# The attention layer of a two-layer graph network: its edge networks' steps in another order, and four waits of GpSimd inside a chunk's gathers

## Chip, cores and metric

One NeuronCore of a Trainium2 chip runs the whole program in one launch. The metric is the device time of one execution in microseconds, the median of the runs shown.

## What is computed

A graph of N = 6250 nodes with D = 64 features and E = 206,250 edges, sorted by target row, goes through two layers, each behind a layer norm and a ReLU: a gated relation layer (`_L0_gnn_ref`), and an attention layer. All is float32. The change touches the attention layer alone; cut to that:

```python
def ssp(x): return softplus(x) - log(2)
row, col = edge_index
W_k = lin(ssp(lin(edge_attr, wkn_w1, wkn_b1)), wkn_w2, wkn_b2)   # the key network, 32 -> 16 -> 16
W_v = lin(ssp(lin(edge_attr, wvn_w1, wvn_b1)), wvn_w2, wvn_b2)   # the value network, 32 -> 16 -> 16
keys_j = lin(W_k[:, None, :] * h_keys[col], wkl_w, wkl_b)
qk_ij = sum(h_queries[row] * keys_j, axis=-1)
alpha = segment_softmax(qk_ij, row, n)                           # over the edges of one row
msg_j = lin(W_v[:, None, :] * h_values[col], wvl_w, wvl_b)
aggr = segment_sum(alpha[:, :, None] * msg_j, row, num_segments=n)
out = lin(ssp(lin(x, cen_w, cen_b) + aggr), out_w, out_b)
```

The kernel folds the linear parts behind the networks into node tables, so that an edge needs the gathered row of its column (keys and values, 128 floats), its network outputs (32 floats) and its row's query.

## The kernel before, in words

The program runs in stages, one behind the other: a front, a sort of the edge records (`sort`, some 130 to 2880 us), the relation layer and its nodes, `attention_layer` (3399 to 5712 us) and `attention_nodes`.

**Tiling.** Each of the 128 partitions holds a run of consecutive edges. They are taken in CHUNKS = 62 chunks of T = 26 edges for each partition. The loop goes over PAIRS = 31 pairs; in each body b = 0, 1 and n = 2i + b. First and last pair are written out, the 29 between are a hardware loop (`loop`, L100). Tiles with [b] are double buffered.

**What a chunk costs each engine in the attention layer.**
- SP loads the chunk's attributes (attr) and query starts (qin), L1376 and L1378.
- GpSimd issues 26 indirect DMAs (L1395), each a gather of 128 rows of kv_table into one column of got[b]. Before the first it waits for s_used (DVE is done with got[b] of chunk n-2), s_idx (the indices of n) and s_w (TensorE has turned the networks' output of chunk n-1). A `sem_inc` on k.s_passed stands behind such waits.
- TensorE computes the networks of chunk n: transposes of flat_attr into p_a (L1411, signal s_at), a product with w1 into p_z (L1416, s_z), one with w2 into p_a again (L1420, s_net), and the turn back into p_w (L1424, s_w). The work is in two halves of 4 and 3 groups of 128 columns; between two steps ACT or DVE has one: ACT's copies to attr_t (L1452), its relu, abs, exp and ln (L1456 to L1460, signal s_soft), DVE's add relu + soft (L1530, s_ssp), ACT's copy with bias to net_t (L1467, s_net_copied).
- DVE takes the chunk through the attention: a scan that spreads queries over edges (L1537), product with the gathered keys (L1545, behind its waits for s_w and s_got), with the key network (L1548), sum by head (L1549), a running maximum (L1557) and differences (below, L1563, signal s_below), value times value network (L1567, s_value), times the weight (L1572, behind its wait for ACT's s_exp), and the scan of the state (L1580, s_state).
- ACT lays out queries (L1437) and marks (L1442), takes exponentials (L1472 to L1475), packs the results (L1479, L1483) and issues their store (L1486).

**Order around the change.** The order on each engine is written by hand. In ACT's body for n stand: lay_out(n+1), networks(n+1) from flat_attr to ln, then finish(n): exponentials, networks_end(n+1), packing, marks(n+1), store. DVE has activated(n+1) behind L1567 and ahead of L1572. TensorE's body for n holds the four steps of chunk n's networks one behind the other.

In the sort stage GpSimd issues 26 scatters for a chunk (L625). From the third chunk on it also waits at each fourth of them for s_dst, a step of TensorE (L623).

## Time and profile before

| | us |
|---|---|
| median of 3 runs | 5864.14 |
| lowest and highest | 5855.48, 5867.09 |
| profiled execution, its own time | 5865.56 |
| its span | 5863.7 |
| granted TensorE clock, mean of the span | 0.531 |
| attention layer, from GpSimd's first gather to DVE's last state scan | 3399.8 to 5709.1 |
| busy in the span: PE, DVE, ACT, GpSimd | 2726.4, 3881.4, 2758.0, 3278.9 |

Times in the profile are microseconds from the start of the span. PE is TensorE, DVE VectorE, ACT ScalarE, POOL GpSimd and SP SyncE; PEld are TensorE's weight loads. A timeline row gives start, length, engine, line, what is written from what, and in brackets the engine's idle time before it with what ended that: an instruction, "issue" where nothing in the profile ended just then, "remote" where a semaphore update arrived that no instruction's end stands close to. Most signals reach their waiter within 0.1 us of the end of the instruction that sends them. Ends of matmuls are modelled.

### The profile page before, as it was taken

To read this page: it belongs to the slowest core of one execution; us is meant where nothing else is said; L and a number is where in the kernel's file an instruction comes from. 1 tells how busy PE (TensorE), PEld (TensorE's weight loads), DVE (VectorE), ACT (ScalarE), POOL (GpSimd) and SP (SyncE) were. 2 spreads that over 40 slices of the span, in tenths; PEclk is the share of its full clock that TensorE was granted. 3 is DMA by queue.
4 is the path that set the end of the run, shared out by engine and by line. 5 is a ranking of instruction groups with operands and counts; after the bars stand their busy time and mean duration, and the time that the engine had idled before them with its cause. 6 is when DMAs were issued, how large, how long until landed. Compare 5 with 4: busy or idle time off the path is not lost. (4 is left out here: it accounts for less than half of the span.)

```text
span 5863.7 us, 79660 instructions
## 1 busy us (share of the span) xinstructions
PE 2726.4 (46%) x21110; PEld 1693.1 (29%) x21111; DVE 3881.4 (66%) x8751; ACT 2758.0 (47%) x5413; POOL 3278.9 (56%) x3388
## 2 busy tenths in 40 slices
PE   7655555555555555555488622322223222222223
PEld 7433333333333333333388511111111111111102
DVE  9867777777777777776599645655556666655552
ACT  3244444444444444444122345655555555555552
POOL 0146565666666565656610266666666666666653
PEclk8555555555555555555577755555555555555555
DMA  5112121212121212121477533433334343433321
GB/s 64 55 54 71 63 71 62 71 63 71 63 71 63 71 63 71 63 71 58 103 160 145 72 103 100 124 110 108 108 103 111 109 110 103 110 108 109 109 79 24
DMA packets 691304, 505.28 MB, mean 86 GB/s; under 512 B 588446, under 2 KB 605214, under 8 KB 691109
## 3 DMA queue, kind: packets, MB, share of 16 engines
q1 hardware_dynamic: 573012, 246.99, 18.2%
q0 software_dynamic: 108736, 196.93, 11.6%
q10 hardware_dynamic: 9360, 59.56, 2.7%
q14 instruction: 172, 1.40, 0.1%
q8 instruction: 24, 0.39, 0.0%
HBM read 289.96 MB, written 213.26 MB: 86 GB/s over the span
## 5 line engine op out<-in xcount | busy, mean ns | idle before, releaser
L625 POOL DMA_INDIRECT records<-rec,place x1612 | 1557.2, 966 | 1306.9 <-issue 451.0
L1395 POOL DMA_INDIRECT got_a<-kv_table,idx_a x1612 | 1539.5, 955 | 762.8 <-issue 691.9
L860 DVE SCALAR_TENSOR_TENSOR same_before<-p_src,src_f,before 128x128 bf16<-128x128 f32 x1612 | 775.0, 535 | 0.0
L711 ACT ACTIVATE lo_away<-p_lo,minus_number 128x512 bf16<-128x512 f32 x434 | 291.2, 671 | 615.5 <-remote 593.6
L668 PE MATMUL p_src<-fields,select 3*128 3x512 bf16 x434 | 248.3, 572 | 687.7 <-DVE same_before L860 512.0
L1411 PE MATMUL p_a<-ident,flat_attr 128*128 128x128 f32 x434 | 123.5, 433 | 930.5 <-issue 447.4
L807 DVE TENSOR_TENSOR picked<-p_look,hi_hot 128x392 f32<-128x392 f32 x434 | 231.5, 533 | 407.5 <-remote 398.2
L1420 PE MATMUL p_a<-relu,w_t 128*128 128x512 f32 x248 | 230.8, 1034 | 463.4 <-issue 332.5
L850 DVE TENSOR_SCALAR dst_hot<-p_dst,number 128x512 bf16<-128x512 f32 x434 | 307.3, 708 | 191.1 <-remote 178.1
L643 PE MATMUL p_look<-table_low,lo_hot_t 128*128 128x98 bf16 x1612 | 410.2, 281 | 0.0
L643 PE MATMUL p_look<-table_rest,lo_hot_t 128*128 128x98 bf16 x1612 | 409.4, 280 | 0.0
L1545 DVE TENSOR_TENSOR prod<-got_a,wide 128x1664 f32<-128x1664 f32 x62 | 117.0, 1888 | 440.2 <-remote 216.3
L643 PE MATMUL p_look<-table,lo_hot_t 128*128 128x98 bf16 x1612 | 402.3, 278 | 0.0
L730 ACT ACTIVATE h_gated<-p_h,gate_s 128x64 f32<-128x64 f32 x1586 | 372.1, 315 | 51.5 <-remote 12.2
L653 PE MATMUL p_h<-window,dst_hot 128*128 128x64 bf16 x4836 | 357.6, 242 | 65.1 <-issue 64.9
L1014 PE MATMUL acc<-high,lo_r 128*128 128x64 bf16 x1708 | 345.4, 244 | 60.0 <-DVE low L1079 40.7
L708 ACT COPY table<-p_place 128x49 f32<-128x49 f32 x434 | 91.7, 211 | 597.0 <-issue 371.6
L1411 PEld LDWEIGHTS p_a<-ident,flat_attr 128*128 128x128 f32 x434 | 75.6, 215 | 978.3 <-issue 824.4
L1014 PE MATMUL acc<-rest_r,lo_r 128*128 128x64 bf16 x1708 | 344.3, 243 | 0.0
L1014 PE MATMUL acc<-low,lo_r 128*128 128x64 bf16 x1708 | 344.2, 243 | 0.0
L653 PEld LDWEIGHTS p_h<-window,dst_hot 128*128 128x128 bf16 x4836 | 312.2, 133 | 54.2 <-issue 53.8
L1014 PEld LDWEIGHTS acc<-high,lo_r 128*128 128x128 bf16 x1708 | 291.3, 171 | 67.6 <-issue 66.3
(377 smaller groups left out, 8443.3 us busy)
## 6 DMA issues: line engine op xcount, KB each, us to landing
sums<-packed_a ACTq DMA_DIRECT2D x62, 936.0 KB
q_starts<-zero_q SPq DMA_DIRECT2D x62, 884.0 KB
rec_r<-records SPq DMA_DIRECT2D x124, 442.0 KB
qin<-q_starts SPq DMA_DIRECT2D x62, 884.0 KB
attr_a<-records SPq DMA_DIRECT2D x62, 442.0 KB
records<-rec,place POOLq DMA_INDIRECT x1612
got_a<-kv_table,idx_a POOLq DMA_INDIRECT x1612
stage<-in_edge_attr SPq DMA_DIRECT2D x61, 416.0 KB
```

Source lines behind the costliest of these rows:

```text
L625: nc.gpsimd.indirect_dma_start(k.records, bass.IndirectOffsetOnAxis(ap=place[b][:, t:t + 1], axis=0), rec[b][:, t, :], None).then_inc(s_se ...
L643: last = nc.tensor.matmul(p_look[qb][:, j * 2 * HI:(j + 1) * 2 * HI], lo_hot_t[qb][:, j * P:(j + 1) * P], part, start=(e == 0), stop=(e == 2))
L653: last = nc.tensor.matmul(p_h[qb][:, j * D:(j + 1) * D], dst_hot[qb][:, j * P:(j + 1) * P], part, start=(e == 0), stop=(e == 2))
L668: nc.tensor.matmul(p_src[:, 0:m * P], k.select[:, NODE, :], rows, start=True, stop=True).then_inc(s_src, 1)
L711: nc.scalar.activation(lo_away[qb][:, 0:m * P], p_lo[:, 0:m * P], ACT.Abs, bias=k.minus_number[:]).then_inc(s_lo_away, 1)
L730: last = nc.scalar.activation(to, p_h[qb][:, j * D:(j + 1) * D], ACT.Copy, scale=gate[b][:, t:t + 1])
L807: v.tensor_tensor(picked[:, 0:n, :, :], p_look[gb][:, 0:n * 2 * HI].rearrange("p (g a h) -> p g a h", a=2, h=HI), bc(group_hot(k, b, g, HI ...
L850: v.tensor_scalar(dst_hot[qb][:, 0:m * P], p_dst[:, 0:m * P], k.number[:], None, ALU.is_equal).then_inc(s_dst_hot, 1)
L860: last = v.scalar_tensor_tensor(same_before[:, first:first + j + 1, :].rearrange("p g e -> p (g e)"), p_src[:, 0:(j + 1) * P], k.src_f[:, ...
L1014: last = nc.tensor.matmul(acc[:, to(t // SUPER)], lo[b][:, :, t], part, start=False, stop=True, skip_group_check=True)
L1395: nc.gpsimd.indirect_dma_start(got[b][:, t, :], None, k.kv_table, bass.IndirectOffsetOnAxis(ap=idx[b][:, t:t + 1], axis=0)).then_inc(s_got ...
L1420: nc.tensor.matmul(p_a[:, 0:c1 - c0], k.w2_t[:], relu[:, c0:c1], start=True, stop=True).then_inc(s_net, 1)
```

## The change

TensorE's steps become four functions of a chunk number m: attributes (the transposes), first_product, second_product and turned (the turn back). The body for n now holds second_product(n+1), attributes(n+2), turned(n+1), first_product(n+2). The banks p_a and p_z become p_n[0] and p_n[1], one for each half, and each is used for all three kinds of output of its half. The prologue computes the networks of chunk 0 and part of those of chunk 1.

ACT's order for n becomes: lay_out(n+1), networks_end(n+1), flattened(n+2), exponentials(n), attributes(n+2), and in finish(n), behind the wait for s_state: marks(n+1), activation(n+2), packing, store. DVE's activated moves from between L1567 and L1572 to ahead of the waits for s_w and s_got, and its one add over 896 columns becomes seven over 128, with s_ssp raised once a half.

GpSimd loses the wait for s_w ahead of a chunk. From the second pair on it waits ahead of gather 4 for s_net of chunk n, ahead of 8 for s_at of n+1, ahead of 13 for s_w of n, and ahead of 18 for s_z of n+1, each with a `sem_inc` on k.s_passed behind it. `follows(i, b, more)` tells whether chunk n + more exists.

```diff
--- before.py
+++ after.py
@@ -1347,7 +1347,7 @@
         relu = tile("relu", [P, GROUPS * P])
         soft = tile("soft", [P, GROUPS * P])
         half = tile("half", [P, 1])
-        p_a, p_z = bank("p_a"), bank("p_z")
+        p_n = [bank(f"p_n{j}") for j in range(2)]
         p_w = banks("p_w", 2)
         wide = banks("wide", 4)
         flat = wide[:, 0:QW * T1]
@@ -1360,6 +1360,10 @@
         s_rec, s_qin, s_got, s_store = ([sem(f"{n}{b}") for b in range(2)] for n in ("s_rec_a", "s_qin", "s_got_a", "s_store_a"))
         records_v, starts_v, sums_v = by_run(k.records), by_run(k.q_starts), by_run(k.sums1)
 
+        def follows(i, b, more):
+
+            return not (isinstance(i, int) and 2 * i + b + more >= CHUNKS)
+
         halves = ((0, 4 * P, 4), (4 * P, GROUPS * P, GROUPS - 4))
 
         with nc.Block() as block:
@@ -1389,9 +1393,18 @@
                         n = 2 * i + b
                         wait(pool, s_used, n - 1)
                         pool.wait_ge(s_idx, n + 1)
-                        wait(pool, s_w, n)
                         pool.sem_inc(k.s_passed, 1)
                         for t in range(T):
+                            if not (isinstance(i, int) and i == 0) and t in (4, 8, 13, 18):
+                                if t == 4:
+                                    pool.wait_ge(s_net, 2 * n + 2)
+                                if t == 8 and follows(i, b, 1):
+                                    pool.wait_ge(s_at, 2 * n + 4)
+                                if t == 13:
+                                    pool.wait_ge(s_w, n + 1)
+                                if t == 18 and follows(i, b, 1):
+                                    pool.wait_ge(s_z, 2 * n + 4)
+                                pool.sem_inc(k.s_passed, 1)
                             nc.gpsimd.indirect_dma_start(
                                 got[b][:, t, :], None, k.kv_table,
                                 bass.IndirectOffsetOnAxis(ap=idx[b][:, t:t + 1], axis=0)).then_inc(s_got[b], 16)
@@ -1400,29 +1413,50 @@
 
             @block.tensor
             def _(pe):
+                def attributes(m):
+                    pe.wait_ge(s_flat, m + 1)
+                    wait(pe, s_net_copied, 2 * m)
+                    for j, (c0, c1, groups) in enumerate(halves):
+                        for g in range(c0 // P, c0 // P + groups):
+                            last = nc.tensor.transpose(p_n[j][:, g * P - c0:(g + 1) * P - c0], flat_attr[:, g * G:(g + 1) * G, :].rearrange("p t c -> p (t c)"), k.ident[:])
+                        last.then_inc(s_at, 1)
+
+                def first_product(m):
+                    for j, (c0, c1, groups) in enumerate(halves):
+                        pe.wait_ge(s_at_copied, 2 * m + j + 1)
+                        nc.tensor.matmul(p_n[j][:, 0:c1 - c0], k.w1_t[:], attr_t[:, c0:c1], start=True, stop=True).then_inc(s_z, 1)
+
+                def second_product(m):
+                    for j, (c0, c1, groups) in enumerate(halves):
+                        pe.wait_ge(s_ssp, 2 * m + j + 1)
+                        pe.wait_ge(s_z_read, 2 * m + j + 1)
+                        nc.tensor.matmul(p_n[j][:, 0:c1 - c0], k.w2_t[:], relu[:, c0:c1], start=True, stop=True).then_inc(s_net, 1)
+
+                def turned(m):
+                    wait(pe, s_value, m)
+                    pe.wait_ge(s_net_copied, 2 * m + 2)
+                    for g in range(GROUPS):
+                        last = nc.tensor.transpose(p_w[:, g * P:(g + 1) * P], net_t[:, g * P:(g + 1) * P], k.ident[:])
+                    last.then_inc(s_w, 1)
+
+                attributes(0)
+                first_product(0)
+                second_product(0)
+                attributes(1)
+                turned(0)
+                first_product(1)
+
                 def body(i):
                     for b in range(2):
                         n = 2 * i + b
-                        pe.wait_ge(s_flat, n + 1)
-                        for j, (c0, c1, groups) in enumerate(halves):
-                            wait(pe, s_at_copied, 2 * n + j)
-                            wait(pe, s_net_copied, 2 * n)
-                            for g in range(c0 // P, c0 // P + groups):
-                                last = nc.tensor.transpose(p_a[:, g * P - c0:(g + 1) * P - c0], flat_attr[:, g * G:(g + 1) * G, :].rearrange("p t c -> p (t c)"), k.ident[:])
-                            last.then_inc(s_at, 1)
-                        for j, (c0, c1, groups) in enumerate(halves):
-                            pe.wait_ge(s_at_copied, 2 * n + j + 1)
-                            wait(pe, s_z_read, 2 * n + j)
-                            nc.tensor.matmul(p_z[:, 0:c1 - c0], k.w1_t[:], attr_t[:, c0:c1], start=True, stop=True).then_inc(s_z, 1)
-                        pe.wait_ge(s_ssp, n + 1)
-                        for j, (c0, c1, groups) in enumerate(halves):
-                            wait(pe, s_net_copied, 2 * n + j)
-                            nc.tensor.matmul(p_a[:, 0:c1 - c0], k.w2_t[:], relu[:, c0:c1], start=True, stop=True).then_inc(s_net, 1)
-                        wait(pe, s_value, n)
-                        pe.wait_ge(s_net_copied, 2 * n + 2)
-                        for g in range(GROUPS):
-                            last = nc.tensor.transpose(p_w[:, g * P:(g + 1) * P], net_t[:, g * P:(g + 1) * P], k.ident[:])
-                        last.then_inc(s_w, 1)
+                        if follows(i, b, 1):
+                            second_product(n + 1)
+                        if follows(i, b, 2):
+                            attributes(n + 2)
+                        if follows(i, b, 1):
+                            turned(n + 1)
+                        if follows(i, b, 2):
+                            first_product(n + 2)
 
                 loop(pe, body)
 
@@ -1441,20 +1475,26 @@
                     act.wait_ge(s_same, n + 1)
                     nc.scalar.copy(factor[:, :, 1:T1], bc(same[b][:], 1, QW)).then_inc(s_keep, 1)
 
-                def networks(n, i, b):
+                def flattened(n, i, b):
 
                     act.wait_ge(s_rec[b], 16 * (i + 1))
                     wait(act, s_at, 2 * n)
                     nc.scalar.copy(flat_attr[:, 0:T, :], attr[b][:, :, 0:EC]).then_inc(s_flat, 1)
+
+                def attributes(n):
+
                     wait(act, s_z, 2 * n)
                     for j, (c0, c1, _) in enumerate(halves):
                         act.wait_ge(s_at, 2 * n + j + 1)
-                        nc.scalar.copy(attr_t[:, c0:c1], p_a[:, 0:c1 - c0]).then_inc(s_at_copied, 1)
+                        nc.scalar.copy(attr_t[:, c0:c1], p_n[j][:, 0:c1 - c0]).then_inc(s_at_copied, 1)
+
+                def activation(n):
+
                     wait(act, s_net, 2 * n)
                     for j, (c0, c1, _) in enumerate(halves):
                         act.wait_ge(s_z, 2 * n + j + 1)
-                        nc.scalar.activation(relu[:, c0:c1], p_z[:, 0:c1 - c0], ACT.Relu, bias=k.b1_c[:])
-                        nc.scalar.activation(soft[:, c0:c1], p_z[:, 0:c1 - c0], ACT.Abs, bias=k.b1_c[:]).then_inc(s_z_read, 1)
+                        nc.scalar.activation(relu[:, c0:c1], p_n[j][:, 0:c1 - c0], ACT.Relu, bias=k.b1_c[:])
+                        nc.scalar.activation(soft[:, c0:c1], p_n[j][:, 0:c1 - c0], ACT.Abs, bias=k.b1_c[:]).then_inc(s_z_read, 1)
                     act.wait_ge(s_z_read, 2 * n + 2)
                     c.then(nc.scalar.activation(soft[:], soft[:], ACT.Exp, scale=-1.0))
                     nc.scalar.activation(soft[:], soft[:], ACT.Ln, bias=half[:], scale=0.5).then_inc(s_soft, 1)
@@ -1464,22 +1504,25 @@
                     wait(act, s_w, n)
                     for j, (c0, c1, _) in enumerate(halves):
                         act.wait_ge(s_net, 2 * n + j + 1)
-                        nc.scalar.activation(net_t[:, c0:c1], p_a[:, 0:c1 - c0], ACT.Identity, bias=k.b2_c[:]).then_inc(s_net_copied, 1)
-
-                def finish(n, i, b):
+                        nc.scalar.activation(net_t[:, c0:c1], p_n[j][:, 0:c1 - c0], ACT.Identity, bias=k.b2_c[:]).then_inc(s_net_copied, 1)
+
+                def exponentials(n):
 
                     act.wait_ge(s_below, n + 1)
                     nc.scalar.activation(add[:, D:QW, 1:T1], below[:], ACT.Exp)
                     nc.scalar.activation(weight, below[:], ACT.Exp)
                     nc.scalar.activation(factor[:, 0:D, :].rearrange("p (h d) t -> p h d t", h=NH), bc(drop[:], 2, HD), ACT.Exp)
                     nc.scalar.activation(factor[:, D:QW, :], drop[:], ACT.Exp).then_inc(s_exp, 1)
-                    if not at_end(i, b):
-                        networks_end(n + 1)
+
+                def finish(n, i, b):
+
+                    act.wait_ge(s_state, n + 1)
+                    if follows(i, b, 1):
+                        marks(n + 1, i + b, 1 - b)
+                    if follows(i, b, 2):
+                        activation(n + 2)
                     wait(act, s_store[b], 16 * i)
                     c.mark(nc.scalar.copy(packed[b][:, :, QW:SW], top[b][:, :, 1:T1].rearrange("p h t -> p t h")))
-                    act.wait_ge(s_state, n + 1)
-                    if not at_end(i, b):
-                        marks(n + 1, i + b, 1 - b)
                     nc.scalar.copy(packed[b][:, :, 0:QW], state[b][:, :, 1:T1].rearrange("p c t -> p t c")).then_inc(s_packed, 1)
                     act.wait_ge(s_packed, n + 1)
                     c.wait()
@@ -1489,17 +1532,27 @@
                 c.begin(0)
                 marks(0, 0, 0)
                 lay_out(0, 0, 0)
-                networks(0, 0, 0)
+                flattened(0, 0, 0)
+                attributes(0)
+                activation(0)
                 networks_end(0)
+                flattened(1, 0, 1)
+                attributes(1)
+                activation(1)
 
                 def body(i):
                     if not at_start(i):
                         c.begin(i)
                     for b in range(2):
                         n = 2 * i + b
-                        if not at_end(i, b):
+                        if follows(i, b, 1):
                             lay_out(n + 1, i + b, 1 - b)
-                            networks(n + 1, i + b, 1 - b)
+                            networks_end(n + 1)
+                        if follows(i, b, 2):
+                            flattened(n + 2, i + 1, b)
+                        exponentials(n)
+                        if follows(i, b, 2):
+                            attributes(n + 2)
                         finish(n, i, b)
                     if not at_end(i):
                         c.end()
@@ -1527,7 +1580,11 @@
 
                 def activated(n):
                     dve.wait_ge(s_soft, n + 1)
-                    nc.vector.tensor_tensor(relu[:], relu[:], soft[:], ALU.add).then_inc(s_ssp, 1)
+                    for j, (c0, c1, groups) in enumerate(halves):
+                        for g in range(groups):
+                            at = slice(c0 + g * P, c0 + (g + 1) * P)
+                            last = nc.vector.tensor_tensor(relu[:, at], relu[:, at], soft[:, at], ALU.add)
+                        last.then_inc(s_ssp, 1)
 
                 def chunk(n, i, b):
                     dve.wait_ge(s_query, n + 1)
@@ -1539,6 +1596,8 @@
                     dve.wait_ge(s_q, n + 1)
                     c.then(nc.vector.tensor_copy(query[1 - b][:, :, 0:1], factor[:, :, T:T1]))
 
+                    if follows(i, b, 1):
+                        activated(n + 1)
                     dve.wait_ge(s_w, n + 1)
                     dve.wait_ge(s_got[b], SCATTERED * (i + 1))
 
@@ -1565,8 +1624,6 @@
                     value = got[b][:, :, D:2 * D]
                     by_head = value.rearrange("p t (h d) -> p t h d", h=NH)
                     nc.vector.tensor_tensor(by_head, by_head, bc(nets[:, :, HD:EC], 2, NH), ALU.mult).then_inc(s_value, 1)
-                    if not at_end(i, b):
-                        activated(n + 1)
                     dve.wait_ge(s_exp, n + 1)
                     dve.wait_ge(s_value, n + 1)
                     nc.vector.tensor_tensor(add[:, 0:D, 1:T1].rearrange("p (h d) t -> p h d t", h=NH), value.rearrange("p t (h d) -> p h d t", h=NH),
```

## Rows read from the trace of the kernel before

**Rows 1.** The page's costliest groups: GpSimd's gathers. Columns: busy, mean ns, idle before.

```profile
L1395 POOL DMA_INDIRECT got_a<-kv_table,idx_a x1612 | 1539.5, 955 | 762.8 <-issue 691.9
```

**Rows 2.** The windows view, steady part of the attention layer. Columns: stretch, length, engines, PEclk.

```profile
3806.00:5584.00 1778.00, 516.75 (x1056) 221.37 (x1056) 1057.98 (x1009) 1004.05 (x1009) 1187.97 (x1248) 0.50 0.40 109
```

**Rows 3.** The timeline of GpSimd: start, length, work, idle time before and its releaser.

```profile
3399.75 0.96 POOL L1395 DMA_INDIRECT got_a<-kv_table,idx_a  x1 [11.44 <-DVE idx_a L1518]
...
4431.95 0.95 POOL L1395 DMA_INDIRECT got_a<-kv_table,idx_a  x1 [0.30 <-issue]
...
4464.11 0.94 POOL L1395 DMA_INDIRECT got_a<-kv_table,idx_a  x1 [0.30 <-issue]
4472.77 0.94 POOL L1395 DMA_INDIRECT got_a<-kv_table,idx_a  x1 [7.72 <-issue]
...
5584.30 0.95 POOL L1395 DMA_INDIRECT got_a<-kv_table,idx_a  x1 [9.46 <-issue]
```

**Rows 4.** The timeline of all engines, chunk 28, second after a stop of GpSimd.

```profile
4453.79 1.73 PE L1424 MATMUL p_w<-ident,net_t 128*128 128x128 f32 x7 [1.14 <-issue]
...
4468.19 1.09 PE L1411 MATMUL p_a<-ident,flat_attr 128*128 128x128 f32 x4 [12.67 <-issue]
...
4472.10 0.59 ACT L1452 COPY attr_t<-p_a 128x512 f32<-128x512 f32 x1 [4.14 <-remote]
4472.18 1.89 DVE L1545 TENSOR_TENSOR prod<-got_a,wide 128x1664 f32<-128x1664 f32 x1 [8.51 <-remote]
```

**Rows 5.** The same view, chunk 27, first after a stop.

```profile
4401.47 1.92 PE L1416 MATMUL p_z<-attr_t,w_t 128*128 128x512 f32 x2
...
4403.48 0.69 ACT L1456 ACTIVATE relu<-p_z,b_c 128x512 f32<-128x512 f32 x1 [1.29 <-PE p_z L1416]
```

**Rows 6.** The same view, chunk 28, half way.

```profile
4438.31 1.62 PE L1416 MATMUL p_z<-attr_t,w_t 128*128 128x384 f32 x2 [1.88 <-ACT soft L1457]
...
4442.46 0.58 ACT L1456 ACTIVATE relu<-p_z,b_c 128x384 f32<-128x384 f32 x1 [4.29 <-remote]
```

**Rows 7.** The same view, sort stage, its second chunk, which has no wait inside.

```profile
311.63 0.96 POOL L625 DMA_INDIRECT records<-rec,place  x1 [34.45 <-ACTq L762]
...
316.46 0.28 PE L643 MATMUL p_look<-table_low,lo_hot_t 128*128 128x98 bf16 x1
...
343.25 0.96 POOL L625 DMA_INDIRECT records<-rec,place  x1 [0.30 <-issue]
348.40 0.57 DVE L807 TENSOR_TENSOR picked<-p_look,hi_hot 128x392 f32<-128x392 f32 x1 [23.92 <-remote]
```

**Rows 8.** The timeline of GpSimd, sort stage: the first scatter of four runs.

```profile
1107.72 0.96 POOL L625 DMA_INDIRECT records<-rec,place  x1 [2.51 <-remote]
...
1120.29 0.96 POOL L625 DMA_INDIRECT records<-rec,place  x1 [2.64 <-remote]
...
1129.98 0.96 POOL L625 DMA_INDIRECT records<-rec,place  x1 [2.40 <-PE p_dst L670]
...
1136.62 0.96 POOL L625 DMA_INDIRECT records<-rec,place  x1 [1.89 <-PE p_dst L670]
```

**Rows 9.** The timeline of DVE behind chunk 28's first gather.

```profile
4433.27 1.89 DVE L1545 TENSOR_TENSOR prod<-got_a,wide 128x1664 f32<-128x1664 f32 x1 [5.48 <-DMA got_a<-kv_table,idx_a]
...
4440.61 1.88 DVE L1567 TENSOR_TENSOR got_a<-got_a,p_w 128x1664 f32<-128x1664 f32 x1
```

**Rows 10.** The view of waits, attention layer: us in total, times, longest.

```profile
DVE relu L1530 <- ACT soft L1460: 167.0, 46, 19.8
```

**Rows 11.** Groups of instructions, attention layer: busy, mean ns, idle before.

```profile
L1530 DVE TENSOR_TENSOR relu<-relu,soft 128x896 f32<-128x896 f32 x62 | 67.8, 1094 | 255.1 <-ACT soft L1460 167.0 <-issue 88.1
...
L1563 DVE TENSOR_TENSOR below_a<-logit_carry,top 128x104 f32<-128x104 f32 x62 | 16.6, 268 | 2.1
```

**Rows 12.** The timeline of all engines, chunk 28: an add of DVE and a gather.

```profile
4446.88 1.09 DVE L1530 TENSOR_TENSOR relu<-relu,soft 128x896 f32<-128x896 f32 x1 [4.39 <-ACT soft L1460]
4447.10 1.70 POOL L1395 DMA_INDIRECT got_a<-kv_table,idx_a  x1 [0.31 <-issue]
```

## The prediction

> **What bounds the kernel now.** I began with the page: 26 gathers for each of 62 chunks make 1,612 issues by GpSimd at L1395, 955 ns each, and the idle time before them is mostly "issue" [rows 1]. The windows view of the steady part of the attention layer, 3806 to 5584 us, is 48 chunks: GpSimd 1187.97 us busy, DVE 1057.98, ACT 1004.05, PE 516.75 [rows 2]. That is 24.7, 22.0, 20.9 and 10.8 us for a chunk. Then GpSimd's own timeline: it begins the layer at 3399.75 and chunk 59 at 5584.30, so 37.03 us for a chunk [rows 3]. Back to back a gather takes 1.25 us (0.95 busy, 0.30 between), 26 of them 32.5. The missing 4.5 us is no steady loss: chunk 27's gathers run into chunk 28's at 4431.95 with 0.30 us between, the last starts at 4464.11, and chunk 29's first only at 4472.77 [rows 3]. After every 52 gathers there is one stop of 7 to 9.5 us. GpSimd's pace sets the stage; what ends that stop sets GpSimd.
>
> **What ends the stop.** The timeline of all engines shows it [rows 4]. TensorE's transposes into p_w (s_w of chunk 28) end at 4455.5. GpSimd and DVE both wait for that semaphore, and both go on only at 4472.2 to 4472.8, DVE after 8.51 us idle "remote" (an update came, but no instruction had ended just then). In the same moment ACT's L1452 starts at 4472.10 after transposes that ended at 4469.3. So work of TensorE is done and its word reaches nobody for up to 16 us. In the first chunk after a stop the word comes at once: matmuls end at 4403.4, ACT starts at 4403.48 [rows 5]. In the second, L1416 ends at 4439.93 and ACT starts at 4442.46, 2.5 us late [rows 6]. No wait of this kind stands behind ACT's or DVE's work.
>
> The sort stage shows the same on another kernel body. Its second chunk issues 26 scatters with no wait inside, 311.63 to 344.2; TensorE's L643 had ended by 316.8, and DVE takes it up at 348.40, 4.2 us after GpSimd is done [rows 7]. Later chunks wait after 4 to 8 scatters, and GpSimd's runs of 8, 6 and 4 start 12.57, 9.69 and 6.64 us apart [rows 8]. With the 74.07 us for 52 of [rows 3] the four lie near one line, 1.02 us for a run and 1.405 us for each gather in it (8 gives 12.3, 6 gives 9.5). I read it so: once a signal of TensorE is held back, it comes out only when GpSimd has been idle for 0.15 us per gather of the run, and a wait on it costs a run its 1.02 us on top.
>
> **The change, part by part.**
> 1. GpSimd's wait on s_w at a chunk's head goes; waits on s_net, s_at, s_w, s_z come at gathers 4, 8, 13 and 18. Queued behind each are the rest of that chunk's gathers, and for the last of them waits DVE's L1545. If the step is done and its signal is out, a wait costs nothing: the one at 4431.95 stands behind a gap of 0.30 us like any other [rows 3]. Are the steps done? Chunk 28's gathers begin at 4431.95, DVE's L1545 of the chunk before at 4433.27, its L1567 ends at 4442.5 [rows 9]; TensorE's turn takes 1.73 [rows 4], so s_w is ready 12.3 us after the first gather, and gather 13 starts at 16.3. s_z comes after ACT's exponentials and copies and L1416's passes (1.92 and 1.62 us, [rows 5, 6]); I put it some 5 us behind s_w, at 17, against gather 18 at 22.5. s_net and s_at come earlier by 4 us or more against theirs, since DVE will be waiting for gathers. So a stop comes only from a held signal.
> 2. second_product for n+1, attributes for n+2, turned for n+1 and first_product for n+2 run in the body of n, a chunk further ahead. In ACT's order the activation of n+2 moves behind the state scan, where L1572's wait on ACT does not see it. The work is the same; two table loads for a chunk stay. DVE's path from one L1545 to the next loses L1530's wait for ACT (167.0 us in 46 chunks, 19.8 at most, [rows 10]) and comes to an estimated 28 us: 22.0 busy [rows 2] and some 6 us of waits for ACT (mark, soft, exponentials). That is worth nothing while GpSimd needs 37, and is needed if GpSimd came down to 32.5.
> 3. L1530, 896 columns in 1,094 ns, becomes seven adds of 128. By that rate and by a 104-column operation's 268 ns [rows 11] they take 1.1 to 1.9 us on DVE, in front of L1545 now, where DVE waits for gathers anyway: nothing, 1.9 at worst if GpSimd ceased to bind. A gather beside L1530 took 1.70 us in place of 0.95 [rows 12]; 0.75 us for a chunk is the most that smaller pieces give back. I take nothing, the two cancelling and the stops setting the rate. SBUF — State Buffer of the Trainium skill (section SBUF: two separate sides) has it that a DVE operation with two SBUF inputs and a GpSimd one that reads SBUF lock each other out for a whole instruction. By that a gather could lose the whole 1.09 us; the row shows 0.75 once, not at each.
> 4. SP's loads wait on s_flat and s_query, whose order on ACT changes, not their count; no DMA is added. The prologue does two chunks' networks and GpSimd's first two chunks have no waits inside. Between 10 us lost and 5 won, once; I take 0.
>
> **The sum.** Everything hangs on how many stops a chunk has, by the line above: one in two chunks 37.05 us, one per chunk 37.55, two 38.56, four 40.6. Today it is one in two. In the first chunk of a run signals came at once, in the second they came late; so a run of much over 26 gathers ends in a held one, and with a wait every 4 to 8 gathers GpSimd meets it at once rather than at the chunk's end. I take between one and two, 1.5: 26 x 1.405 + 1.5 x 1.02 = 38.06, 1.03 more than 37.03. The first two chunks have no waits inside, so 60 x 1.03 = +62 us. The sum is made against the profiled run, 5865.6 (span 5863.7 and 1.9 around it): 5927.4. The median of the runs, 5864.14, is 1.4 below that run, so I name 5926.
>
> **The rivals.**
> - **No signal is held: GpSimd back to back.** For it: after a stop signals were prompt for a whole chunk [rows 5], GpSimd now pauses its queue four times a chunk, and DVE (28) and ACT (21) fit below. Against it: in [rows 4] the queue had been waiting and the signal still stayed away until the engine had been idle for 7 us. It needs 32.5 us a chunk: (37.03 - 32.5) x 62 = 281 less, 5583; with a stop in one run of three or so, or late starts, up to 5750. Chance 0.27, with its partial forms. TensorE: Matmul & The Clock Gate of the Trainium skill (section The cost: per-tile semaphore tail) prices a matmul's semaphore increment at 26.3 ns behind a tail of about 25 ns, with nothing that depends on other engines; by it this rival would be the forecast, and [rows 4, 7] disagree with it by 4 to 16 us.
> - **Every wait is a stop, as in the sort stage** [rows 8]. Decides if a signal is held in most runs of six gathers. 40.6 us a chunk, +222: 6086. For it: the sort's signals are late in runs of 4. Against it: the attention layer's are not in the first 26. Chance 0.13.
> - **One stop in two chunks, as now.** The held signal is the same s_w, caught at gather 13 and not at the head; 37.05 a chunk, nothing changes: 5855 to 5875. Chance 0.10.
> - **The waits at the forecast's rate**, one or two stops for a chunk: 5885 to 5990. Chance 0.50.
>
> **How the numbers follow.** Faster by over 0.2% (12 us, about what a measurement here can tell from no change) is the first rival and a few of the forecast's edges: 0.29. Same: 0.10. Slower: 0.61. Left out of the range are the purest form of the first rival and the worst of the second: 5630 to 6080; the slower cases alone would span 5885 to 6086.
>
> **What would show it.** L1395's starts: stops per chunk, and run length against time on the line 1.02 + 1.405 n. Forecast right: stops of 3 to 6 us at gathers 4, 8, 13 or 18, most at one place; the stop at each second chunk's head gone; DVE's L1545 still waiting for gathers; L1572's wait for ACT gone. First rival: gaps of 0.30 us through whole chunks, and DVE no longer waiting "remote". Wrong altogether: a run far off the line, a stop that a late step of TensorE explains (its matmul ends just before), or DVE's path at over 33 us.

## The result, and the profile after

| | before | after |
|---|---|---|
| median of 20 runs each | 5864.13 | 5876.82 |
| lowest and highest | 5848.01, 5879.48 | 5860.05, 5890.16 |
| ratio, 95% interval | | 1.0027 [1.0017, 1.0036] |
| profiled execution, its own time and span | 5865.56, 5863.7 | 5890.16, 5888.4 |
| layer, first gather to end of the last state scan | 3399.75 to 5709.08: 2309.3 | 3410.09 to 5734.38: 2324.3 |

The kernel is slower, by 12.7 us, where the forecast had 62. The layer itself is 15.0 longer in the profiled runs. All that lies ahead of it also moves with no edit there: the layer's first gather is 10 us later here, and between 3379 and 3473 in the profiles of the experiments on like chips. So times of the layer are read from its own first gather on.

The page's groups after (columns as in [rows 1]):

```profile
L1408 POOL DMA_INDIRECT got_a<-kv_table,idx_a x1612 | 1526.1, 947 | 791.1 <-issue 492.1
...
L1433 PE MATMUL p_n<-relu,w_t 128*128 128x512 f32 x248 | 206.8, 989 | 745.0 <-DVE relu L1586 524.9
...
L1604 DVE TENSOR_TENSOR prod<-got_a,wide 128x1664 f32<-128x1664 f32 x62 | 117.0, 1888 | 587.6 <-DMA got_a<-kv_table,idx_a 516.9
```

The windows view of 48 chunks, to be set against [rows 2] (columns as there):

```profile
3835.00:5612.00 1777.00, 463.84 (x1056) 238.15 (x1056) 1075.39 (x1292) 983.83 (x1008) 1177.18 (x1244) 0.55 0.40 108
```

GpSimd's gathers keep it busy 13 us less (1526.1 against 1539.5), the idle time before them is 28 us more (791.1 against 762.8), and 48 chunks take the same time, 1777 against 1778. DVE waits for gathers (516.9 us), as the prediction said. Its idle time ahead of the product with the weight, which stands behind the wait for ACT's s_exp, fell from 147 to 31 us, where the prediction had that wait gone. What GpSimd waits for is in the view of waits, 3430 to 5720 (us in total, times, longest):

```profile
DVE prod L1604 <- DMA got_a<-kv_table,idx_a: 516.9, 51, 16.5
...
POOL got_a L1408 <- remote: 265.6, 58, 8.8
...
ACT relu L1496 <- remote: 112.0, 33, 11.4
ACT attr_t L1489 <- remote: 107.0, 24, 7.8
...
POOL got_a L1408 <- PE p_n L1433: 18.6, 2, 18.3
```

58 stops end "remote", that is with a held signal, and one of 18.3 us with work of TensorE. GpSimd's timeline shows the kinds: a stop in each chunk in the first third, then mostly one or two in every second chunk:

```profile
3630.53 0.94 POOL L1408 DMA_INDIRECT got_a<-kv_table,idx_a  x1 [4.41 <-remote]
3667.34 0.94 POOL L1408 DMA_INDIRECT got_a<-kv_table,idx_a  x1 [4.51 <-remote]
...
5284.85 0.94 POOL L1408 DMA_INDIRECT got_a<-kv_table,idx_a  x1 [6.90 <-remote]
5294.10 0.94 POOL L1408 DMA_INDIRECT got_a<-kv_table,idx_a  x1 [3.31 <-remote]
```

From 3630.53 to 3667.34 there are 26 gathers and one stop: 36.81 us, 1.416 for each. The prediction's line gives 37.55. In the kernel before, the 25 runs of 52 gathers from 3733.06 to 5584.30, with one stop each, cost 74.05, 1.424 for each gather. After, 52 gathers with three stops, from 3742.25 to 3816.34, cost 74.09; the line gives 76.12. **In this layer and on these chips the added stops cost nothing.** The held signals are as large as before: for the stop that ends at 5284.85 GpSimd waits for transposes that ended at 5272.74.

The difference lies at the start. Heads of chunks 0, 3 and 60 on GpSimd are at 3399.75, 3506.88, 5616.80 before and at 3410.09, 3527.43, 5641.33 after. So the first three chunks take 107.1 and 117.3, **10.2 more**; the next 57 take 2109.9 and 2113.9, 4.0 more, 37.02 against 37.09 for a chunk. The rest, 0.8, is at the end. Two more traces of the changed kernel (f1 and g1 below) have 117.4 and 117.2 for the first three chunks and 36.92 and 37.11 for a chunk behind them. So the loss at the start repeats, and the 4.0 is no more than these traces differ among themselves; of the kernel before there is one trace. The 10.2 is this stop (the timeline of all engines, after):

```profile
3473.93 0.48 ACT L1489 COPY attr_t<-p_n 128x384 f32<-128x384 f32 x1 [7.76 <-remote]
...
3478.80 0.94 POOL L1408 DMA_INDIRECT got_a<-kv_table,idx_a  x1 [0.30 <-issue]
...
3487.31 0.69 ACT L1496 ACTIVATE relu<-p_n,b_c 128x512 f32<-128x512 f32 x1 [11.36 <-remote]
...
3492.95 1.50 DVE L1586 TENSOR_TENSOR relu<-relu,soft 128x128 f32<-128x128 f32 x7 [12.58 <-ACT soft L1500]
...
3493.91 3.35 PE L1433 MATMUL p_n<-relu,w_t 128*128 128x512 f32 x4 [17.80 <-DVE relu L1586]
...
3498.05 0.94 POOL L1408 DMA_INDIRECT got_a<-kv_table,idx_a  x1 [18.30 <-PE p_n L1433]
```

GpSimd has issued 56 gathers without a wait and stands ahead of gather 4 of chunk 2 for s_net. What is held is not s_net but two earlier signals, s_at's second half and s_z, on ACT's side. ACT gets s_z only 8.5 us after the last gather's start, and behind it stand ACT's activation, DVE's adds and the second product: 10.7 us of real work, to 3498.05.

### The profile page after: what moved, and what is told of

Same layout as the page of the kernel before. It is cut to its first block and busy times, and to the rows that moved or that the text cites. A ratio compares the mean times of both kernels' runs of the same rounds, so it can differ in the third digit from the quotient of the medians.

```text
span 5888.4 us, 80298 instructions
## 1 busy us (share of the span) xinstructions
PE 2656.3 (45%) x21110; PEld 1713.9 (29%) x21111; DVE 3909.9 (66%) x9123; ACT 2735.1 (46%) x5413; POOL 3260.6 (55%) x3388
## 5 line engine op out<-in xcount | busy, mean ns | idle before, releaser
L625 POOL DMA_INDIRECT records<-rec,place x1612 | 1552.5, 963 | 1323.5 <-issue 444.8
L1408 POOL DMA_INDIRECT got_a<-kv_table,idx_a x1612 | 1526.1, 947 | 791.1 <-issue 492.1
L1433 PE MATMUL p_n<-relu,w_t 128*128 128x512 f32 x248 | 206.8, 989 | 745.0 <-DVE relu L1586 524.9
L1604 DVE TENSOR_TENSOR prod<-got_a,wide 128x1664 f32<-128x1664 f32 x62 | 117.0, 1888 | 587.6 <-DMA got_a<-kv_table,idx_a 516.9
L1439 PE MATMUL p_w<-ident,net_t 128*128 128x128 f32 x434 | 108.7, 428 | 536.5 <-issue 295.5
L1433 PEld LDWEIGHTS p_n<-relu,w_t 128*128 128x128 f32 x248 | 72.8, 324 | 866.0 <-DVE relu L1586 580.0
```

What stands on the lines that cost most here:

```text
L625: nc.gpsimd.indirect_dma_start(k.records, bass.IndirectOffsetOnAxis(ap=place[b][:, t:t + 1], axis=0), rec[b][:, t, :], None).then_inc(s_se ...
L1408: nc.gpsimd.indirect_dma_start(got[b][:, t, :], None, k.kv_table, bass.IndirectOffsetOnAxis(ap=idx[b][:, t:t + 1], axis=0)).then_inc(s_got ...
L1433: nc.tensor.matmul(p_n[j][:, 0:c1 - c0], k.w2_t[:], relu[:, c0:c1], start=True, stop=True).then_inc(s_net, 1)
```

## The experiments

The prediction's theory, P: a stop costs GpSimd 1.02 us on top of 1.405 for each gather. What was found instead, A: on these chips GpSimd cannot keep 1.25 us for a gather in the long run; it falls behind a slower rate, and a stop only makes up for that and costs nothing. The text calls this the backlog. Each batch had its own runs of the kernel before beside it.

### What does a chunk cost without any wait for TensorE?

**e1**, the kernel before with networks for chunk 0 alone:

```diff
-                        wait(pool, s_w, n)
...
-                loop(pe, body)
+                body(0)
...
-                            networks(n + 1, i + b, 1 - b)
+                            flattened(n + 1, i + b, 1 - b)
```

> The kernel before, but TensorE computes the edge networks of chunk 0 alone and every chunk uses that output; ACT's and DVE's network steps of later chunks are left out, and so is each wait on TensorE after chunk 0. Held signals (theory H: GpSimd can issue a gather each 1.25 us, and only a signal of TensorE that is held back stops it): chunks 32.5 to 33 us apart, the layer some 250 us shorter, time near 5610. Rate (theory R: a gather really costs about 1.41 us on average, whoever waits): chunks still 36.7 us apart, time near 5860.

Measured: 5814.09, ratio 0.9913 [0.9871, 0.9954]. Seven chunks go at 32.5 us, then every chunk at 36.4, to the end (3699.72 to 5591.82 for 52). There is no stop; the gathers themselves stretch, and are 1069 ns in the mean. In the timeline of GpSimd and DVE:

```profile
4448.17 1.25 POOL L1394 DMA_INDIRECT got_a<-kv_table,idx_a  x1 [0.46 <-issue]
...
4451.69 0.29 DVE L1543 COPY query<-wide 128x68 f32<-128x68 f32 x1
...
4456.71 1.79 POOL L1394 DMA_INDIRECT got_a<-kv_table,idx_a  x1 [0.30 <-issue]
4458.81 1.11 POOL L1394 DMA_INDIRECT got_a<-kv_table,idx_a  x1 [0.30 <-issue]
...
4465.25 1.89 DVE L1548 TENSOR_TENSOR prod<-got_a,wide 128x1664 f32<-128x1664 f32 x1 [13.27 <-DMA got_a<-kv_table,idx_a]
```

So 32.5 us was out of reach on these chips, with or without held signals: after some 180 gathers of 1.25 us the rate is 1.40. DVE idles from 4452 to 4465 while gathers last up to 1.79 us, so this stretching is not DVE's. SBUF — State Buffer of the Trainium skill (section SBUF: two separate sides) lets a DVE operation with two inputs in SBUF hold up a GpSimd one that reads SBUF; at 4456.71 no DVE operation runs.

**e7** is e1 with rows of 256 bytes in place of 512 (from h_table); **e8** is e1 with SP's loads for chunks 0 and 1 alone. Each was executed once.

```diff
...
-                                got[b][:, t, :], None, k.kv_table,
+                                got[b][:, t, 0:D], None, k.h_table,
...
```
```diff
...
-                loop(sp, body)
+                body(0)
...
```

> As e1_one_network, but each gather takes rows of 64 floats from another table (256 bytes in place of 512; the value half of the tile stays at zero, and the result of the attention is left wrong). e1 ran 7 chunks 32.5 us apart and then 36.4, its gathers stretched. Theory R (something behind the gather takes 1.40 us for each, whatever its size, and can be some 20 gathers behind): 36.4 us for a chunk again, from the same chunk on. Theory B (bytes or traffic on the DMA engines): 32.5 us throughout.

> As e1_one_network, but SP loads attributes and query starts for chunks 0 and 1 alone; later chunks use them again, so that 1.3 MB for each chunk, with 3,328 small descriptors, are gone and ACT's stores remain. R: 36.4 us for a chunk again. B (the loads slow the gathers' descriptors or their landing): 32.5 us throughout, layer some 220 us shorter than e1's.

Measured: 5816.47 and 5803.96, 36.4 us a chunk in both from chunk 7 on (layers of 2251.3 and 2249.8 us; e1's is 2247.3). The windows view, 4000 to 5600, e7 and then e8 (columns as in [rows 2]; e1's GB/s is 110):

```profile
4000.00:5600.00 1600.00, 0.00 (x0) 0.00 (x0) 922.66 (x880) 520.57 (x396) 1234.67 (x1142) 0.50 0.34 86
```
```profile
4000.00:5600.00 1600.00, 0.00 (x0) 0.00 (x0) 917.96 (x875) 520.58 (x396) 1236.15 (x1142) 0.50 0.25 73
```

The traffic falls by a fifth and a third and the pace stays: 1142 gathers in each, as e1 has 1144. Neither bytes nor SP's loads set it. What all three have alike is the number of gathers and of rows in each.

The backlog is not in the gathers' own transfers either. In e1 it would be 27 us by gather 180 (180 times 0.15). But in the DMA packets of the traces a gather's first data packet starts 1.66 us behind the start of its issue in the kernel before and in the changed one, 1.80 in e1, and its last ends 2.20, 2.21 and 2.31 us behind it (medians of 1612 gathers), and never more than 5.4. What is behind by that much, no run shows.

### What are GpSimd's waits worth?

**e2** is the changed kernel without its four waits, **e5** the kernel before without its wait at the chunk's head.

```diff
-                            if not (isinstance(i, int) and i == 0) and t in (4, 8, 13, 18):
...
```
```diff
-                        wait(pool, s_w, n)
```

> The changed kernel without GpSimd's four waits, new order of the networks kept; GpSimd waits only for s_used and s_idx at a chunk's head. H: held signals stay away until GpSimd runs dry by itself, runs of 52 gathers and more, stops at the heads of chunks, DVE and ACT late by up to 20 us; chunks 37 to 40 us apart, time 5865 to 6000. If the waits only cost (rival): 5640 to 5800, faster than both kernels.

> The kernel before without GpSimd's wait on s_w at a chunk's head. H: DVE waits for the same held signal, so GpSimd runs out of free buffers about a chunk later; runs of 52 to 78 gathers, stops longer, chunks still 36.7 to 37.5 us apart, time 5855 to 5890. If the head's wait itself makes the stop (rival): chunks 33.3 us apart as in the layer's first ones, time near 5660.

Measured: 6195.01, 1.0583 [1.0508, 1.0658], and 6115.51, 1.0451 [1.0371, 1.0530], 42.5 and 41.1 us a chunk. Both expectations, 6000 and 5890 at most, missed. GpSimd then runs 78 gathers and stops for DVE at every third head (timelines of GpSimd, e2, then e5):

```profile
4404.28 0.94 POOL L1398 DMA_INDIRECT got_a<-kv_table,idx_a  x1 [29.57 <-DVE idx_a L1561]
```
```profile
4441.97 0.94 POOL L1394 DMA_INDIRECT got_a<-kv_table,idx_a  x1 [25.20 <-DVE idx_a L1517]
```

TensorE's signals are held through the whole run, the chain of networks stands still at ACT, and DVE waits for it (e2, view of waits):

```profile
DVE relu L1576 <- ACT soft L1490: 785.8, 57, 28.8
...
ACT relu L1486 <- remote: 646.1, 64, 22.5
```

So the one wait at the head is worth 246 us in the order of before, and the four inside some 310 in the new one (6195.01 against 1.0027 times this batch's 5869.07 for the kernel before). Here held signals do cost: where GpSimd never waits for TensorE, their lateness reaches DVE and comes back to GpSimd as stops of 25 to 30 us, far more than the backlog of 78 gathers, 12 us (78 times 0.15).

### Do held signals themselves cost time?

**e9** and **e10**: the kernel before with a memset of GpSimd behind each gather, of 1 and of 64 columns (e10 was executed once).

```diff
...
+                            nc.gpsimd.memset(pad[b][:, t * PAD:(t + 1) * PAD], 0.0).then_inc(s_pad, 1)
```

> The kernel before, with a GpSimd memset of one column behind each gather, so that gathers start further apart (some 1.35 to 1.5 us in place of 1.25). If held signals come from GpSimd running ahead of what takes 1.40 us a gather, then at 1.40 us or more nothing is held: no remote waits, no stop at each second chunk, chunks 26 times the spacing (35.1 to 39 us) apart. At 1.40: 36.4 us, time near 5830, faster than both kernels; at 1.5: 39, time near 5985. If signals are held by the mere presence of gathers: stops remain, on top of the wider spacing, 39 to 41 us, time over 5985.

> As e9_pad_1 with a memset of 64 columns, some 0.05 us more for each gather. Spacing theory: no stop, chunks 26 times the spacing apart, 1.3 us more than e9's if that has none either; if e9 is still below 1.40 us for a gather, fewer or shorter stops than there.

Measured: 5868.37, 0.9996 [0.9981, 1.0011], and 5870.55. GpSimd's timeline in e9:

```profile
4430.47 0.95 POOL L1399 DMA_INDIRECT got_a<-kv_table,idx_a  x1 [0.19 <-issue]
4431.41 0.11 POOL L1402 MEMSET pad<- 128x1 f32 x1
4431.72 0.95 POOL L1399 DMA_INDIRECT got_a<-kv_table,idx_a  x1 [0.19 <-issue]
...
4435.07 0.94 POOL L1399 DMA_INDIRECT got_a<-kv_table,idx_a  x1 [1.04 <-issue]
```

The memset fits in the gap of 0.30 us, and gathers stay 1.25 apart. The stops of 8 us are gone, and small pauses of about 1 us stand all over in their place. DVE's product waited 216.3 us "remote" and 196.0 for gathers in the kernel before; in e9 no wait of it ends "remote" (view of waits, the kernel before, then e9):

```profile
DVE prod L1545 <- remote: 216.3, 28, 9.3
DVE prod L1545 <- DMA got_a<-kv_table,idx_a: 196.0, 25, 10.9
```
```profile
DVE prod L1550 <- DMA got_a<-kv_table,idx_a: 640.3, 48, 14.8
```

A chunk takes 37.07 us as ever. Of e9's forecast the end of the held signals came, but not the way to it: the memset did not move the gathers apart, and the chunk did not fall to the 36.4 us of e1. **In the order of before, as long as GpSimd stops now and then, held signals come and go without changing the time of a chunk.** That is the plainest evidence for A against P.

### The stop at the start

**e3** is the changed kernel with its waits from chunk 0 on, **e13** (run again as f2 and g2) with them from chunk 1; f1 and g1 are the changed kernel itself once more.

```diff
-                            if not (isinstance(i, int) and i == 0) and t in (4, 8, 13, 18):
+                            if t in (4, 8, 13, 18):
```
```diff
-                            if not (isinstance(i, int) and i == 0) and t in (4, 8, 13, 18):
+                            if not (isinstance(i, int) and i == 0 and b == 0) and t in (4, 8, 13, 18):
```

> The changed kernel with the four waits in the first pair of chunks too. The stop of 18 us at gather 4 of chunk 2 shows that signals were held through the first 52 gathers. H: that stop goes, the layer is 12 to 18 us shorter, time 5858 to 5866, level with the kernel before. If the stop has another cause (the prologue's longer chain on ACT): it stays and the time is 5877.

Measured: 5906.73, 1.0075 [1.0038, 1.0112], where 5858 to 5866 was expected; the first three chunks take 124.3 us. The stop is now in chunk 0 and nearly as long (GpSimd's timeline):

```profile
3445.04 0.95 POOL L1408 DMA_INDIRECT got_a<-kv_table,idx_a  x1 [16.97 <-PE p_n L1433]
```

> The changed kernel, nothing edited. In the last batch of runs the kernel before took 5027 us and not 5864 to 5873, gathers stayed at 1.25 us and TensorE's signals were never held. If that is so here too: theory A (the held signals and the gathers' slow rate are all that the change's waits run into) gives 32.5 us a chunk without a stop, 4990, ratio 0.992 to 0.994; rival B (the prologue's two networks cost 10 us or more anywhere) 5000. If it is as in the earlier batches: 5877 against 5864 to 5873, ratio 1.001 to 1.004, with the stop of 18 us at chunk 2.

> The changed kernel with its waits from chunk 1 on. Under the conditions of the first batches: theory A (the change's loss is the one stop of 18 us at chunk 2) gives 37.1 us a chunk without that stop, 9 to 15 us below the changed kernel of this batch. Rival B (the loss is spread, or the prologue's): no less than the changed kernel. Under those of the last batch: 4990 once more, equal to the changed kernel, since no signal is held at chunk 2 there.

> The changed kernel once more, nothing edited, since one batch of it stood at 1.0008 [0.9974, 1.0042] with runs that scattered by 1%. Under the conditions in which the kernel before takes 5027 us: 32.5 us a chunk, 4990, ratio 0.992 to 0.994, as both of its near relatives did. Under the others: ratio 1.001 to 1.004 and the stop of 18 us at chunk 2.

> The changed kernel with its waits from chunk 1 on, once more. Theory A (the loss is the stop at chunk 2): 5 to 15 us below the changed kernel of this batch where the kernel before takes some 5870; equal to it within 2 us where that takes 5027. Rival B (no part of the loss is that stop): within 3 us of it in either.

Measured, the changed kernel and then e13: 5922.68 and 5907.76, ratios 1.0008 [0.9974, 1.0042] and 0.9974 [0.9935, 1.0012]; in the next batch 5896.05 and 5874.97, 1.0030 [1.0000, 1.0060] and 1.0006 [0.9970, 1.0041]. The medians favour e13 by 15 and 21 us, but the intervals overlap, and the traces don't bear it out: the first three chunks take 117.4 and 115.8 us in the one pair, 117.2 and 118.1 in the other, since e13 stops in chunk 1 (g2, GpSimd's timeline):

```profile
3443.32 0.94 POOL L1408 DMA_INDIRECT got_a<-kv_table,idx_a  x1 [13.99 <-PE p_n L1433]
```

The expectation that the stop falls below 9 us missed. Moving the wait moves the stop.

**h1** is the changed kernel with e9's memset of 1 column.

> The changed kernel with a memset of GpSimd (128x1) behind each gather. Where the kernel before takes some 5870: moving the first wait (e3, f2, g2) moved the stop of 11 to 18 us at the layer's start but did not remove it; in each, ACT gets a held s_z, and ACT's, DVE's and TensorE's work up to s_net stands behind that. Theory A (the stop at the start is a held signal with a chain behind it, and the memsets keep signals from being held, as in the kernel before): the stop falls to 4 us or less, the first three chunks take 98 to 108 us and not 117, the steady part stays at 37.0 to 37.1, the layer 2306 to 2314 us, ratio 0.998 to 1.001. Rival B (the prologue's chain itself, two networks with four table loads, is too long for the wait at gather 4): the stop stays at 9 us or more, ratio 1.001 to 1.004.

Measured: 5916.82, 1.0025 [0.9988, 1.0062]. The stop is 8.05 us. In spite of the memsets one signal was held, and long: TensorE's first product for chunk 1 ended at 3488.59, and ACT took it up at 3509.46 (the timeline of all engines):

```profile
3509.46 0.69 ACT L1501 ACTIVATE relu<-p_n,b_c 128x512 f32<-128x512 f32 x1 [22.41 <-remote]
...
3548.80 0.95 POOL L1412 DMA_INDIRECT got_a<-kv_table,idx_a  x1 [8.05 <-PE p_n L1438]
```

The same kernel on the chip of the next section (e11) shows the start without any held signal: the same product is taken up at once, and gather 4 of chunk 2 has no stop (the timeline of all engines):

```profile
2862.15 0.69 ACT L1501 ACTIVATE relu<-p_n,b_c 128x512 f32<-128x512 f32 x1 [0.99 <-PE p_n L1432]
...
2907.58 0.94 POOL L1412 DMA_INDIRECT got_a<-kv_table,idx_a  x1 [0.19 <-issue]
```

DVE's first state scan ends 71.6 us after the first gather in h1 and 50.6 in e11. From there a chain leads to s_net: ACT's marks and activation(2), DVE's adds, the second product. It takes 14 us in h1, with 1.3 of waiting for one more late signal, and 11.6 in e11, where it ends 8 us ahead of the gather. So the chain alone stops nothing. The changed order puts it ahead of the wait at gather 4, and a signal held before it or in it becomes a stop of GpSimd. Neither forecast came (4 us or less, 9 or more; the first three chunks take 115.0 us, not 98 to 108): the stop is of A's kind, but A's premise, that the memsets keep every signal from being held, was wrong. h1's layer is the shortest of all that compute everything on these chips, 2301.0 us with 36.77 for a chunk (before: 2309.3), but the total does not show a gain; with one trace that stays open.

### Order or waits, and a chip without the backlog

**e4** (again f3) is the kernel before, order and all, with four waits inside for its own steps in place of the one at the head; **e11** is the kernel of h1.

```diff
...
-                        wait(pool, s_w, n)
...
+                                if t == 4:
+                                    pool.wait_ge(s_at, 2 * n + 2)
+                                if t == 8:
+                                    pool.wait_ge(s_z, 2 * n + 2)
+                                if t == 13:
+                                    pool.wait_ge(s_net, 2 * n + 2)
+                                if t == 18:
+                                    pool.wait_ge(s_w, n + 1)
```

> The changed kernel, with its four waits from chunk 1 on and not from chunk 2. In the changed kernel GpSimd runs 56 gathers without a wait, ACT gets s_z of chunk 2 only at 3487.31, 8 us after the last of them, and the wait is for s_net, with ACT's and DVE's work between (11 us more): one stop of 18. Theory A (all of the change's loss is this one stop, a held signal caught two steps ahead of the one waited for): with a wait for s_z ahead of gather 18 of chunk 1 the stop falls to the size of the others (under 9 us), the steady part stays at 37.1 us for a chunk, and the kernel comes out at 5862 to 5868, 9 to 15 us below the changed kernel, level with the kernel before. Rival B (the layer has to do two chunks' networks at its start, wherever GpSimd waits): as much is lost in other stops, 5875 to 5880.

> The kernel before, with its own order on every engine, and in place of the wait at a chunk's head the four waits inside, each for the step of TensorE due then in that order: s_at, s_z, s_net, s_w of the same chunk ahead of gathers 4, 8, 13, 18, from the third chunk on. It tells the waits from the new order. Theory A (GpSimd cannot keep more than 1.40 to 1.42 us a gather, and stops that let its backlog drain are free whatever their number; the order is worth nothing): 37.0 to 37.4 us a chunk, 5865 to 5885. Rival B (the change's order was needed for these waits: in the order of before a step is not done when the gather is due): stops that a step of ACT or DVE ends, over 38 us a chunk, 5920 or more. The prediction's line gives 38.06 us a chunk at one and a half stops, 5926.

> The changed kernel with one small memset of GpSimd (128x1) behind each gather. In the kernel before this took away nearly all the held signals of TensorE and moved the time by nothing (0.9996). Theory A (held signals cost nothing in the steady part, since the gathers' own rate binds; they cost only at the stop of 18 us): steady part 37.0 to 37.2 us a chunk, the stop at chunk 2 under 12 us, 5860 to 5875. Rival B (the waits of the change are what keeps the rate at 37.1 where 36.4 is the floor, by held signals): 36.4 us a chunk and 5825 to 5840.

This batch ran on another chip, so that forecasts made for the first ones can't be judged by it. The kernel before took 5026.89 there (5025.37 to 5029.09), e13 4990.12, ratio **0.9927 [0.9913, 0.9940]**, e11 4989.82, 0.9926 [0.9911, 0.9941], e4 5166.93, **1.0280 [1.0264, 1.0295]**. In e13 GpSimd's idle time is smaller in the sort too (the page; 1323.5 us at L625 in the changed kernel above):

```profile
L625 POOL DMA_INDIRECT records<-rec,place x1612 | 1552.2, 963 | 750.9 <-issue 467.4
L1408 POOL DMA_INDIRECT got_a<-kv_table,idx_a x1612 | 1524.9, 946 | 502.5 <-issue 473.6
```

A scatter and a gather last as long as ever (963 and 946 ns). But 1612 gathers follow each other at 1.25 us to the last, 32.52 a chunk, no signal is held, and nothing waits "remote". The first three chunks take 97.5 us in e13 and in e11, 78 gathers at 1.25: the start of the new order costs nothing here either. In the new order the four waits cost nothing. In the order of before they do: e4 stops in every chunk for the second product, which stands behind DVE's one add (e4, view of waits and timeline):

```profile
POOL got_a L1408 <- PE p_a L1433: 193.2, 60, 3.3
```
```profile
3909.49 1.08 DVE L1543 TENSOR_TENSOR relu<-relu,soft 128x896 f32<-128x896 f32 x1
...
3915.98 0.94 POOL L1408 DMA_INDIRECT got_a<-kv_table,idx_a  x1 [3.29 <-PE p_a L1433]
```

> The kernel before with four waits inside, each for its own order's step. In the last batch it lost 2.8%: ahead of gather 13 each chunk stood 3.0 us for TensorE's second product, which waited for DVE's add, 35.5 us a chunk. Under the conditions of the first batches, theory A (stops only let the backlog drain, the gathers' rate of 1.40 us binds) gives 37.0 to 37.4 us a chunk, a ratio of 1.000 to 1.003: the 3 us stop is hidden in the slower rate. Rival B (the stop for a step that is really late comes on top): 39 or more, ratio above 1.02.

Back under the first conditions e4 had 5920.62, 1.0033 [0.9996, 1.0069], with 37.14 us a chunk (view of waits):

```profile
POOL got_a L1408 <- remote: 130.2, 35, 5.8
POOL got_a L1408 <- PE p_a L1433: 116.5, 42, 4.4
```

The same late step, which costs 2.8% on the one chip, is hidden on the other: by A, because each stop only makes up for what GpSimd is behind anyway. The 37.14 us is what theory A expected.

The sort, which no run edits, differs between the chips in the same way. In the kernel before its chunks are 41.6 us apart, and from the fourth chunk on GpSimd stops 243 times for over 0.8 us, 127 times until TensorE's p_dst ends and 101 times "remote"; in e13 they are 32.97 apart with one such stop, of 1.1 us. So the stops for p_dst go too where nothing is held. Of the 901 us between the changed kernel and e13, 572 are in the sort, 290 in the attention layer and 39 behind it; the 532 us between sort and layer are the same.

> The kernel before with the networks of all chunks but the first left out, so that GpSimd waits for nothing of TensorE. Under the conditions of the first batches it was bound by gathers that stretched to 1.40 us apart from chunk 7 on, 36.4 us a chunk. Under those of the last batch, theory A (the stretching and the held signals go together, with the gathers' own sustained rate) gives 32.5 us a chunk to the end and 4985 to 4995; rival B (the stretching comes of this kernel's own traffic and is there under any condition): again 36.4 us a chunk, some 200 us more.

It repeated e1: 5837.89, 0.9914 [0.9878, 0.9950], 36.39 us a chunk. The faster chip was not met again. So e1 and the changed kernel with nothing edited have no run there; its near relatives e13 and e11 do. Of the kernel before there are times from there but no trace. Whether it is the chip or something in its condition is open.

## Why the prediction was wrong in size

- **That GpSimd paces the layer and TensorE's signals are held**: right under the conditions of the prediction. **Direction**: right, but by luck. The sum had all of the loss in step 1, and it was in step 4, which was taken as 0. The time is nearest to the third rival, that nothing changes (5855 to 5875, chance 0.10).
- **Step 1, the failing step: the line.** 1.02 us for a run came from the sort's runs of 8, 6 and 4 scatters [rows 8] and one run of 52; the attention layer had a single length. Two of the four stops in [rows 8] end with p_dst, a step of TensorE that had just finished, and not with a held signal, so they were no price of a hold alone. In the sort short runs with a stop do cost more for each scatter (1.66 us in runs of 4, 1.62 in runs of 6, 1.55 in runs of 8); why, no run shows. In the attention layer the 1.02 us isn't there. Measured: 26 gathers with a stop 36.81, where the line has 37.55; 52 with three 74.09, where it has 76.12; 37.09 for a chunk over 57 chunks, where the sum had 38.06. The step's +62 is +4.0, within the scatter of the traces. Its count of stops, 1.5 for a chunk, was too high too (58 "remote" in 60 chunks), but at no price for a stop the count doesn't matter.
- **"The missing 4.5 us is no steady loss"** was the reading behind it, and it is the reverse: 36.4 us is what 26 gathers cost in the long run (e1), and 1.25 us is what it gives on credit. When the stop comes is up to the held signal, after 52 gathers in the kernel before, where e1 goes through some 180 before it slows down; how long it is there, 7.4 to 9.5 us in most, fits 0.15 us for each of the 52.
- **The first rival** was priced at 32.5 us a chunk and given 0.27. Under these conditions no kernel tried came near it, and e1, without a wait for TensorE, has 36.4: its layer is 62 us shorter than before's, and 281 were counted on. Where the backlog does not exist, e13 has 32.5, but there the kernel before is only 37 us slower, 0.6 for a chunk; without a trace of it, what it loses them to is not shown.
- **Step 2**, the order is worth nothing under these conditions: right (f3, the old order with four waits, has 37.14 us a chunk, the new order 37.09). On the other chip it decides whether the four waits win 37 us or lose 140.
- **Step 3**, seven adds net nothing: DVE's adds take 1.50 us in place of 1.09 and DVE waits for gathers behind them, as said. No run tried the one add in the new order.
- **Step 4**, the prologue, taken as 0 within −5 to +10: it was 10.2 of the 15.0 by which the layer is longer. On the other chip, without held signals, e13's start has no such stop. "GpSimd's first two chunks have no waits inside" was noted, but not that the first wait behind them is for a step three engines away from the signal that would be held.
- **What would have shown it** from the profile of before: the slope of the prediction's own line. 1.405 us for a gather, over 1.25, was read as the time that a hold takes to clear; it is the price of a gather.

## What to carry to other kernels

When an engine stops after each so many issues, first ask what its issues cost in the long run, with a kernel that has no stops at all; a stop may be the place where a backlog drains, and then adding stops or spreading them out does not move the time. Where signals can be held, a wait for a step with two engines' work behind the held signal adds the hold and the work, as the stop at the start shows; a wait for the held step itself might avoid that, but no run tried it there. No wait at all was worst. And a verdict of 0.3% belongs to the conditions under which it was taken: here the change that costs 0.3% on some chips has a near relative (e13) that gains 0.7% on another.

## What the runs showed of the hardware

- Indirect gathers of 128 rows are issued at 1.25 us for some 180 in a row, then at 1.40, with the same rate at 256 and 512 bytes a row (e1, e7, f4). Their data packets do not fall behind (2.31 us behind the issue in the median of e1, 5.4 at most). On the faster chip 1612 go at 1.25 (e13). What sets 1.40, and why kernels with networks stay at 36.8 to 37.1 us a chunk and not 36.4, is open.
- While that backlog stands, signals of TensorE reach other engines late, up to 16 us in [rows 4] and ACT's waits of this kind last up to 22.5 us in e2; a memset of 0.11 us between gathers (e9) removes nearly all of it at the same rate of gathers, but in h1 one signal was 21 us late all the same. No run shows why. TensorE: Matmul & The Clock Gate of the Trainium skill (section The cost: per-tile semaphore tail) has nanoseconds for that signal: e13 agrees with it, where no wait ends "remote"; the kernel before does not.
- The kernel before takes 5027 us on one chip, 14 to 15% less than the 5864 to 5906 on the others. Busy times are alike (GpSimd 3259.4 us in e13, 3260.6 in the changed kernel; DVE 3896.3, 3909.9); the difference is idle time, 862 of 901 us of it (changed kernel against e13) in the sort and the attention layer, in each of which GpSimd issues 1612 indirect DMAs.
